# A graph network kernel: edge records, movers and the node table reordered by one-hot products on TensorE

## The reference, cut to what matters

```python
msg = h[row] * norm[:, None]
out = jax.ops.segment_sum(msg, col, num_segments=N)
...
h_neigh = jax.ops.segment_sum(h[src], dst, num_segments=n) / deg
rst = h @ W_self[l] + h_neigh @ W_neigh[l] + b[l]
```

## Time and profile before

| | us |
|---|---|
| median of 3 runs | 2899.13 (2894.58 to 2900.2) |
| the profiled execution | 2908.8 |
| its span | 2907.1 |
| start of the first layer in it | 172.63 |

### The profile page before, as it was taken

How to read it: one execution, slowest core, us unless ns; L and a number is a source line. 1 busy time by engine, 2 the same in 40 slices (tenths; PEclk the granted TensorE clock), 3 DMA queues, 4 the chain that set the end, 5 groups by cost and what they waited for, 6 DMA issues and landing times. The chain is left out here.

```text
span 2907.1 us, 45066 instructions
## 1 busy us (share of the span) xinstructions
PE 2448.1 (84%) x13348; PEld 1424.1 (49%) x13348; DVE 1899.1 (65%) x4585; ACT 1509.1 (52%) x2234; POOL 1200.4 (41%) x1984
## 2 busy tenths in 40 slices
PE   0437988799879999899997969979999997998954
PEld 0424554344444445444553537756666664444443
DVE  7624887688668876899873436647888887223343
ACT  6524765445334533455334756648888876232270
POOL 5656874336333332455544521114444444001155
PEclk9998998999999999999998989989999999999975
DMA  7443542378658797766553332223333343101178
GB/s 201 164 153 107 162 147 95 108 186 206 129 115 203 202 172 151 226 220 224 191 173 122 102 99 70 80 92 118 122 122 122 133 148 127 38 1 51 49 269 299
DMA packets 379311, 414.18 MB, mean 142 GB/s; under 512 B 198240, under 2 KB 237573, under 8 KB 376206
## 3 DMA queue, kind: packets, MB, share of 16 engines
q1 hardware_dynamic: 350510, 337.43, 39.6%
q0 software_dynamic: 28640, 74.78, 8.7%
HBM read 172.55 MB, written 198.32 MB: 128 GB/s over the span
## 5 line engine op out<-in xcount | busy, mean ns | idle before, releaser
L218 PE MATMUL s_ps_z<-s_w,slots 128*128 128x512 f16 x2844 | 636.8, 381 | 8.0 <-DMA s_w<-split_self 7.8
L218 PEld LDWEIGHTS s_ps_z<-s_w,slots 128*128 128x128 f16 (+1 forms) x2844 | 278.8, 98 | 323.4 <-DMA s_w<-split_self 8.2
L1649 ACT ACTIVATE s_g<-s_g,s_rn 128x512 f32<-128x512 f32 x237 | 169.7, 716 | 226.8 <-POOL s_rn L1508 226.8
L1508 POOL TENSOR_TENSOR s_rn<-s_em,minus_half 128x1 f32<-128x1 f32 x237 | 178.9, 755 | 219.4 <-DVE s_em L1577 211.3
L1558 DVE SCALAR_TENSOR_TENSOR s_g<-s_ps_z,s_f,s_bias 128x512 f32<-128x512 f32 x237 | 177.9, 751 | 107.3 <-PE s_ps_z L218 94.2
L2578 PE MATMUL z_ps_z<-slots,z_w 128*128 128x512 f16 (+1 forms) x960 | 213.1, 382 | 7.8 <-DMA z_w<-split_root 7.8
L2445 PE MATMUL u_ps_z<-slots,u_w 128*128 (+2 forms) x1920 | 215.9, 273 | 0.0
L2445 PEld LDWEIGHTS u_ps_z<-slots,u_w 128*128 128x128 f16 x1920 | 187.1, 99 | 22.4
L2547 DVE BATCH_NORM_STATS2 z_stats<-slots 128x6 f32<-128x512 f32 (+1 forms) x76 | 52.2, 687 | 187.0 <-ACT slots L2564 187.0
L1568 DVE SCALAR_TENSOR_TENSOR s_junk<-s_g 128x512 f32<-128x512 f32 x237 | 164.5, 694 | 4.1
L218 PE MATMUL s_ps_z<-s_wn,s_aT 128*128 128x512 f16 x720 | 165.2, 379 | 1.8 <-DVE s_aT L1392 1.8
(11 more groups left out here) (395 smaller groups left out, 5620.0 us busy)
## 6 DMA issues: line engine op xcount, KB each, us to landing
h_rows<-s_g SPq DMA_DIRECT2D x237, 256.0 KB
x_rows<-q_x SPq DMA_DIRECT2D x79, 256.0 KB
s_halves<-x_rows SPq DMA_DIRECT2D x79, 256.0 KB
x_rows<-s_halves SPq DMA_DIRECT2D x79, 256.0 KB
u_x<-x_rows SPq DMA_DIRECT2D x79, 256.0 KB
x_rows<-u_x SPq DMA_DIRECT2D x79, 256.0 KB
h_rows<-u_h SPq DMA_DIRECT2D x79, 256.0 KB
f_x<-x_rows SPq DMA_DIRECT2D x79, 256.0 KB
```

Of the source, the lines that this page charges most:

```text
L218: ins = nc.tensor.matmul(out_ap, a(c), w[:, part * size + c * n:part * size + (c + 1) * n], start=first and c == 0 and m == 0, stop=stop a ...
L1508: nc.gpsimd.tensor_tensor(out=self.rn[b][:, :], in0=self.em[b][:, :], in1=minus_half[:, :], op=POW).then_inc(self.s_rn, 1)
L1649: nc.scalar.activation(self.g[b][:, :], self.g[b][:, :], ACT.Relu, scale=self.rn[v.buf(2)][:, 0:1]).then_inc(self.s_h, 1)
```

## The change

Three groups of indirect transfers give way to products with one-hot matrices, and the tables in DRAM behind them (`rec_d`, `mover_d`, `node_d`) are gone.

- **Records.** VectorE builds `rec_p` (row in the tile, 125 x 20*128, f32) and `rec_tv` (tile, times each of three values). Twenty f32 products add up to `ps_list`, the sorted records.
- **Movers.** The same in bf16 with `mover_p` and `mover_tv`, into `ps_found`.
- **Picking by order.** The order of a place is split into two digits. The first is spread over a diagonal (`spread`) and broadcast over the partitions by five f32 products of 512 columns with a matrix of ones; a comparison with the partition's number gives `found`; twenty products with the list of movers and a product with the one-hot of the second digit give the mover.
- **The table of nodes** comes from twenty f32 products of `home_p` and `home_t` in PSUM; `node_i` and `out_i` are written in `prepare()`.
- **Magnitudes.** Ten of the twelve matrices are summed on ScalarE; VectorE keeps `update` and `out`. The transpose of the table of magnitudes now stands in TensorE's program behind the order of the places and the first two broadcasts, and all steps to `up` stand in VectorE's program behind `spread`. The first four low halves follow behind the picking.
- **Selections** are stored in four parts, the first two between the stores of the halves.

```diff
-            FIRST_LOWS, FIRST_HIGHS, RING = 4, 6, 5
-            HALF_SUMMED = ("conv", "edge", "root", "aggr")
+            FIRST_LOWS, FIRST_HIGHS = 4, 6
+            EXACT = ("update", "out")
...
-                for t in range(ET):
-                    nc.gpsimd.indirect_dma_start(
-                        mover_d[:, :], bass.IndirectOffsetOnAxis(ap=mover_u[:, t:t + 1], axis=0),
-                        zone_id[:, t:t + 1], None, bounds_check=ZONE - 1, oob_is_err=False).then_inc(s_mover_out, 16)
...
-                for q in range(EQ):
-                    nc.gpsimd.indirect_dma_start(
-                        rec_d[:, :], bass.IndirectOffsetOnAxis(ap=pos_u[0:EP, q:q + 1], axis=0),
-                        rec[0:EP, q, :], None).then_inc(s_rec, 16)
...
+                one_hots(rec_p, place, P, a).then_inc(s_rechot, 1)
+                link(one_hots(rec_t, tile_no, ET, a))
+                for v in range(3):
+                    nc.vector.tensor_tensor(
+                        out=rec_tv[a, :].rearrange("p (q v t) -> p q v t", v=3, t=ET)[:, :, v, :],
+                        in0=rec_t[a, :].rearrange("p (q t) -> p q t", t=ET),
+                        in1=vals[a, v, :].unsqueeze(2).to_broadcast([EP, EQ, ET]), op=MUL).then_inc(s_rechot, 1)
+                link(one_hots(mover_t, mover_b, ET))
...
+                one_hots(mover_p, mover_a, P).then_inc(s_mhot, 1)
...
+                whole_part(order_a[:, :], order_w[:, :], order[:, :], ET)
+                nc.vector.tensor_tensor(out=spread.rearrange("p (t n) -> p t n", n=P),
+                                        in0=order_a[:, :].unsqueeze(2).to_broadcast([P, ET, P]),
+                                        in1=ident[:, :].unsqueeze(1).to_broadcast([P, ET, P]), op=MUL).then_inc(s_spread, 1)
...
+                dve.wait_ge(s_maxT, 1)
...
+                for i in range(ET * P // D):
+                    dve.wait_ge(s_bcast, i + 1)
+                    nc.vector.tensor_scalar(out=found[:, i * D:(i + 1) * D], in0=ps_sel[i % 2][:, :], scalar1=part[:, 0:1],
+                                            scalar2=None, op0=ALU.is_equal).then_inc(s_found, 1)
...
+                one_hots(home_p, home_a, P).then_inc(s_homes, 1)
+                link(one_hots(home_t, home_b, FT))
+                dve.wait_ge(s_pick, 2)
...
+                times_row(home_t, home_t, moved, FT).then_inc(s_homes, 1)
+                for k in range(FIRST_LOWS):
+                    low_half(k)
+                dve.wait_ge(s_node, 1)
...
+                for q in range(EQ):
+                    ins = nc.tensor.matmul(ps_list[:, 0:3 * ET], rec_p[0:EP, q * P:(q + 1) * P],
+                                           rec_tv[0:EP, q * 3 * ET:(q + 1) * 3 * ET], start=q == 0, stop=q == EQ - 1)
...
+                broadcast(0)
+                broadcast(1)
+                pe.wait_ge(s_max, len(EXACT))
+                pe.wait_ge(s_sum, NU - len(EXACT))
+                nc.tensor.transpose(ps_max[0:NU, 0:P], mx[:, :], ident[:, :]).then_inc(s_maxT, 1)
...
+                for k in range(len(jobs)):
+                    store_split(k)
+                    if k in (8, 10):
+                        store_sel(k // 2 - 4)
+                store_sel(2)
```

More of the change, by code:

```diff
@@ L312, in prepare @@
             stored = pair("w", "out", 4)
[L313 to L315 removed]
+            (s_in, s_cast, s_key, s_sign, s_hot, s_count, s_sum, s_col, s_tri, s_rechot, s_rec, s_dcol, s_lineT, s_line, s_lines,
+             s_three, s_flag, s_mflag, s_order, s_morder, s_mplace, s_mhot, s_mlist, s_spread, s_bcast, s_found, s_pick, s_homes,
+             s_node, s_init, s_degree, s_dis, s_link, s_base, s_selT, s_turn, s_sel, s_selout, s_vec, s_vecpart, s_vecout, s_bn,
              s_bnT) = sems(
[L317 to L318 removed]
+                "g", "in cast key sign hot count sum col tri rechot rec dcol lineT line lines three flag mflag order morder mplace "
+                "mhot mlist spread bcast found pick homes node init degree dis link base selT turn sel selout vec vecpart vecout bn "
                 "bnT")
[L320 removed]
             block = ctx.enter_context(nc.Block())
@@ L384, in _ @@
                 nc.gpsimd.memset(tri[:, :], 1.0).then_inc(zid, 1)
+                nc.gpsimd.memset(beyond[:, :], float(NOWHERE)).then_inc(zid, 1)
+                count(node_n[:, 1:FT], P, P - DUMMY, 1)
+                count(node_n[:, 0:1], 0, 0, 1).then_inc(zid, 1)
                 nc.gpsimd.memset(half[:, :], -0.5)
@@ L394, in _ @@
                 count(tile_base[:, :], 0, 0, EPT)
[L395 to L398 removed]
+                count(part[:, :], 0, 0, 1)
+                count(part_t[:, 0, :], 0, 0, 1)
+                count(part_t[:, 1, :], 1, 0, 0)
+                pool.wait_ge(zid, 5)
                 count(home_id[0:1, 0:HEAD], 1, 0, 0).then_inc(s_col, 1)
```

345 lines of the change are left out of this document (181 added, 164 removed).

## The result

| | before | after |
|---|---|---|
| median, four runs each (us) | 2896.86 (2893.61 to 2900.2) | 2878.55 (2877.36 to 2881.69) |
| the profiled execution | 2908.8 | 2881.69 |
| its span | 2907.1 | 2879.9 |

The ratio is 0.9938, with a 95% interval from 0.9921 to 0.9956: 18.3 us faster. The forecast was 10.1 us, and 2878.55 lies under the low end of its range. The two profiled executions differ by more still, 27.2 us; that of the kernel after is one of its four runs, that of the kernel before (2908.8) lies outside the range of its four. Where these three numbers part is the question of this study.

What follows compares the result with a forecast made beforehand. It took the preparation, a chain of small steps ending in GpSimd's late DRAIN, as the bound. -9.8 us there and -0.3 us in the next phase made -10.1, from 2899.1 to 2889.0 us; range 2883 to 2896.

Steps and rivals of the forecast that it cites:

- Part 1: Preparation up to the records: one-hots, reductions and twenty f32 products at 0.43 us each, records ready at 58.1 us.
- The tie with VectorE's reductions: In the preparation, TensorE's records' products and VectorE's two remaining reductions both end at 58.1 us.
- Part 2: From the records to the scales: magnitudes' transpose waits behind two broadcasts, scales at 81.2 us instead of 68.1.
- Part 3: From the scales to the node table: broadcasts, comparisons, picking, home products; selection loop starts at 106.7 us, 6.5 later.
- the found products: Twenty 20-column products with the list of movers, behind the broadcasts: from 87.3 to 91.8 us at full clock.
- full clock throughout: Rival for TensorE in the preparation: broadcasts at 0.93 us, home products hidden, loop at 101.1, time 2883 us; chance 0.15.
- half clock throughout: Rival for TensorE in the preparation: found products end at 95.8, time 2891 us; chance 0.55 together with the main case.
- Part 4: Selection loop unchanged at 49.5 us, then a shorter tail: next phase at 162.8 us, 9.8 earlier.
- the last rival: End of the preparation: GpSimd's DRAIN due to something other than indirect transfers, 2897 us; chance at most 0.02.
- The removed work in `gcn_layer()`, -0.3: Next phase: GpSimd loses a memset, a select and a wait before its first gather, 0.3 us gained.
- late stores: Rival before the selection loop: slower 1 MB stores or missed hand-overs cost some 6 us more, 2895 us; chance 0.22.
- dear f32 products: Rival for the preparation's f32 products: 0.90 us each, 18 instead of 8.5 us a group, 2915 us; chance 0.06.

Runs made afterwards that it cites:

- records_twice: Changed kernel with the twenty products that reorder the records done twice; 0.9982 of the kernel before.
- before_again: The kernel before, unchanged, run for a second profile; 2890.21 us, one run.
- sums_only: The kernel before with only six of VectorE's eight reductions moved to ScalarE as sums; 0.9988 of the kernel before.
- after_again: The changed kernel, unchanged, run for a second profile; 2871.02 us, one run.
- reductions_back: Changed kernel with the six reductions back on VectorE, all else as changed; 0.9999 of the kernel before.
- The other two comparisons: Changed kernel, unchanged, timed again beside the kernel before in two later experiments; 0.9947 and 0.9961.
- after_timed: Changed kernel, unchanged, timed in five rounds as a baseline; 0.9947 of the kernel before, 2892.63 against 2908.18 us.
- scales_first: Changed kernel with the magnitudes' transpose and the chain to the scales moved ahead of the spread and broadcasts; 0.9945 of the kernel before.
- bf16_broadcast: Changed kernel with the five broadcasts of 512 columns in bf16 instead of f32; 0.9934 of the kernel before.
- improved: Changed kernel with early scales, bf16 broadcasts and the node table read out in the selection loop's fifth step; 0.9921, later 0.9922, of the kernel before.

## Why the prediction was wrong in size

The direction, the mechanism and the cause of each part stood. Going by the forecast's own steps (start or end in us, forecast and profile):

```
ranks read                          42.94   42.88
TensorE starts the records          49.4    49.09
records ready                       58.1    57.9
count starts                        60.1    59.46
order read                          69.8    68.9
magnitudes turned                   76.8    76.03
scales ready                        81.2    79.50
last comparison done                88.0    85.4
picking starts                      93.5    90.8
low halves                      96.5-104.1  93.75-101.3
home products done                 105.3   102.7
selection loop                     106.7   104.07
last store issued                  156.2   153.62
next phase                         162.8   158.67
```

- **Part 1 was right.** The spacing of the records' products, the main unknown, was 0.44 us (0.43 taken), and records_twice confirms it. The tie with VectorE's reductions came out within 0.2 us. The count is 0.6 us early, in small terms that each were a little high.
- **Part 2: "From the last magnitude to ScalarE's first high half is 4.4 us"** was too long. From the transpose's start to ScalarE it was 4.23 us in the kernel before (63.89 to 68.12), and is 3.47 us now (76.03 to 79.50). Some 0.2 us of that is TensorE's small product, which VectorE waited 0.69 us for and now 0.48. The rest are single operations of the chain that were stretched before, as the one at 67.53 below (0.54 us; its like takes 0.17 us now). GpSimd was issuing its transfers then, and the two other profiles in which it was gave 3.85 (before_again) and 3.99 us (sums_only); those without gave 3.47 (after_again) and 3.67 us (reductions_back, no operation stretched). That GpSimd's transfers stretch them is the likely reading; no run tests it alone. Another 0.2 us were counted in the step to the order, whose row (L654) stands one operation behind the read-out. With the 0.6 us of part 1 that makes the scales 1.7 us early.

```profile
67.44 0.17 DVE L588 TENSOR_SCALAR w_inv<-w_ex 128x12 int32<-128x12 int32 x1
67.53 0.54 DVE L590 TENSOR_SCALAR up<-w_ex 128x12 int32<-128x12 int32 x1
```

- **Part 3: "three more broadcasts at 1.8"** was the next one. They took 4.28 us together; the clock rose within them, and the last comparison ended 0.9 us sooner behind the scales. This part of the miss is a matter of the execution: in the three other profiles of the changed kernel the same three took 4.50, 5.46 and 4.76 us, and the one below is the forecast's 5.4.

```profile
80.12 5.46 PE L794 MATMUL g_ps_sel<-slots,g_ones 128*128 128x512 f32 x6 [2.85 <-DVE slots L694]
```

- That the found products would run at full clock behind them was right (4.54 us for twenty), and that the home products would not (8.79) too. So the rival of full clock throughout fell, and that of half clock throughout as well. The loop started **2.6 us** earlier than forecast.
- **Part 4: "4.6 us" for a 1 MB store, "then come 0.8 of SyncE's other waits"** was the largest single miss. From the last issue to SyncE's end it took 3.8 us instead of 5.4. Two things were wrong. The 0.8 was counted twice: the 4.6 us ran from a store's issue to its landing, while the 12.4 of the row is a wait that began 0.7 us behind the large store's issue, and behind the landing SyncE has nothing left (landed at 157.33, branch at 157.4). And the 4.6 was the price of another store, that of `edge`. The lines are one `edge` store (issued at 96.78) and the last quarter of the selections in the changed kernel, both with GpSimd silent (KB, us from issue to landing):

```profile
split_edge<-w_parts SPq DMA_DIRECT2D x1, 1024.0 KB, 4.4
selections<-slots SPq DMA_DIRECT2D x1, 960.0 KB, 3.7
```

  GpSimd's traffic is not the reason, as one might think from the moment of the forecast's row: the `edge` store freed ScalarE after 4.46 us in the changed kernel (96.78 to 101.24) and 4.58 before. That makes **1.6 us**, and the stage gained 14.0 instead of 9.8 us.
- **GpSimd's DRAIN.** That the tail would go was right, and it did not stay as the last rival had it. That the DRAIN is simply due to indirect transfers did not hold: one late transfer leaves 0.14 us of DRAIN, and takes 5.0 us to land instead.
- **The removed work in `gcn_layer()`, -0.3,** is not to be seen: GpSimd's first gather comes 0.93 us behind the phase's start, at 159.60, as before (0.91 at 173.54). Nor could it be, beside a scatter of 10 us.
- **The sum.** With the stage as it came out, it would have been 2899.1 - 14.0 = 2885.1 us, inside the range. The remaining 6.5 us down to 2878.55 are 2.3 us by which the median of before came out lower in the four runs, and 4.3 us by which the first comparison exceeds the stage. The other two comparisons gave 15.6 and 12.2 us, so it is within what medians of this kernel scatter by. The forecast took all behind the stage in one profiled execution as fixed; it is not fixed to better than 10 us, and 14 more in the last stage. So 4.2 us of the miss are terms of the sum (1.7 the scales, 0.9 the broadcasts, 1.6 the tail), and what carried the result out of the range beyond them is scatter and the baseline.
- **The range** (2883 to 2896) held bounds for the clock and for late stores, all on the start of the loop, and next to nothing for the tail's landing or for the baseline's own spread.

Of the rivals, "late stores" and "dear f32 products" fell: ScalarE waited 10.67 and 2.67 us for stores before the loop, but only the fifth and sixth high half hung on that, which nothing asked for.

The Trainium skill (TensorE: Matmul & The Clock Gate, LDWEIGHTS) gives 107 ns for a load of 128 columns without naming the clock. Here a pass (weights and 20 to 60 columns) took 213 ns at the 1.2 GHz level and 114 ns at the 2.4 GHz level, so the page's figure fits the upper level alone, and the trace's was the right one for the sum.

## What to carry to other kernels

Take the price of a store from one of its own size and shape, from issue to landing, and count that stretch once: here a neighbour's price and a wait inside it made 1.6 us. A chain of small operations read beside GpSimd's transfers (4.23 us) can be shorter without them (3.47); take the range downward for it. Moving work off an engine that waits anyway gives nothing to the stage (sums_only) and gives all of it (13 us) once the wait is gone: undo a part on the new kernel as well as trying it on the old. And before a difference between two profiles is put down to a change, profile each kernel twice: here 5 and 15 us of the difference of 27, and 7 us the other way, were not the change's.

## What the runs showed of the hardware

- **What TensorE did before its clock rose.** 17.3 us of 60-column f32 products without a gap stayed at 0.43 us each, so at the 1.2 GHz level, and the selection loop read 0.50. In the first profile of the changed kernel the clock fell to 0.50 at 79.9, after one small product since 76.5, and rose at 83.4, within the three 512-column f32 broadcasts; in after_timed it rose at 86.0, in scales_first at 78.0 within five of them. The twenty products behind took 0.23 us each. With the broadcasts in bf16, the twenty behind took 0.43 us again. The Trainium skill (TensorE: Matmul & The Clock Gate, The HAM clock gate) says that sustained work releases the clock; records_twice is sustained, and did not.
- **The granted clock reads 1.00 ahead of its first record.** In bf16_broadcast and improved that is the whole preparation, though every f32 product there has the 1.2 GHz price. In the changed kernel the records begin at 76.5, and the selection loop reads 0.50. Durations tell the level there, the column does not, and neither does the mean clock of a run (0.936 in the changed kernel, 0.951 in bf16_broadcast).
- **Small scattered writes and large stores can hold each other up:** twenty indirect writes in and behind the selection loop took a 1 MB store from 3.9 to 20.8 us and the end of the stage 20 us back. GpSimd's node table before the change, reads and writes in turn, did nothing of the kind to stores of the same size (3.9 to 4.6 us in before_again).
- **The last stage has two durations,** 120.3 and 133 to 135 us, at 343 and 306 GB/s, for one program; its kind changed with the session and its chip, not with the kernel.
